# Two batches of keys and values made in the first routed block, its router taken from raw rows, and third attention's first inputs loaded one stage sooner

## The reference: four layers of gated attention and gated feed-forward

```python
x = x + tanh(g_xattn[0]) * L0_xattn(norm(x), ctx, ctx, mask, wq, wk, wv, wo, bo)   # 16 heads of 16
x = x + tanh(g_ffn[0])   * L0_ffn(norm(x), ...)                                   # routed in depth
x = x + tanh(g_xattn[1]) * L1_xattn(norm(x), ctx, ...)
x = x + tanh(g_ffn[1])   * L1_ffn(norm(x), ...)                                   # 8 experts, one each row
x = x + tanh(g_xattn[2]) * L2_xattn(norm(x), ctx, mask, Wq, bq, Wk, bk, Wv, bv, Wo, bo)  # 16 heads of 64
x = x + tanh(g_ffn[2])   * L2_ffn(norm(x), ...)                                   # 16 experts, four each row
x = x + tanh(g_xattn[3]) * L3_xattn(ctx, norm(x))
x = x + tanh(g_ffn[3])   * L3_ffn(norm(x), ...)
```

```python
weights = (x @ router_w)[..., 0] + router_b[0]        # x is norm(x) here
topv, topi = top_k(weights, 16); sel_idx = sort(topi[:, :15])
hn = rmsnorm(x_sel, ln1); q, k = rope(hn @ wq), rope(hn @ wk); ...
x2 = x1 + gelu(rmsnorm(x1, ln2) @ w1) @ w2            # x1 = x_sel + attention
```

## Time and profile before

| | |
|---|---|
| median of 3 runs | 1598.7 us |
| lowest and highest | 1589.78 and 1600.38 us |
| the profiled execution | 1599.66 us |
| its span, first to last instruction | 1597.9 us |
| mean granted TensorE clock | 0.921 |
| PE, PEld, DVE, ACT, POOL busy | 87%, 72%, 53%, 48%, 27% of the span |

### The profile page before, as it was taken

How to read it: one execution, slowest core, us unless ns; L and a number is a source line. 1 busy time by engine, 2 the same in 40 slices (tenths; PEclk the granted TensorE clock), 3 DMA queues, 4 the chain that set the end, 5 groups by cost and what they waited for, 6 DMA issues and landing times. The chain is left out here.

```text
span 1597.9 us, 32065 instructions
## 1 busy us (share of the span) xinstructions
PE 1393.7 (87%) x10658; PEld 1155.8 (72%) x10658; DVE 850.3 (53%) x2171; ACT 767.9 (48%) x1905; POOL 424.3 (27%) x578
## 2 busy tenths in 40 slices
PE   8999878889999999987999999999999998401588
PEld 5888645677799997766888878789999996400355
DVE  4888665766422223005666653832222274688887
ACT  3666453420344435544677673345555522430277
POOL 1000000012122210002333331256666644431141
PEclk9999999899799999998999997889999999755799
DMA  3000020673211126436344432012222343421001
GB/s 108 21 20 15 5 93 1 210 271 64 64 34 39 35 80 208 165 152 215 111 129 143 143 82 93 1 57 94 92 92 93 87 172 128 112 19 10 0 14 40
DMA packets 114518, 140.17 MB, mean 88 GB/s; under 512 B 37072, under 2 KB 93152, under 8 KB 114272
## 3 DMA queue, kind: packets, MB, share of 16 engines
q1 hardware_dynamic: 91872, 85.86, 17.3%
q0 software_dynamic: 11136, 28.93, 6.4%
q10 hardware_dynamic: 11392, 23.86, 4.3%
HBM read 99.96 MB, written 37.49 MB: 86 GB/s over the span
## 5 line engine op out<-in xcount | busy, mean ns | idle before, releaser
L3673 PEld LDWEIGHTS L2f_bank<-L2f_xT,L2f_w_tile 128*128 128x128 f32 x1264 | 154.0, 192 | 7.5 <-ACT L2f_xT L3741 3.5
L3673 PE MATMUL L2f_bank<-L2f_xT,L2f_w_tile 128*128 128x128 f32 x1264 | 154.7, 276 | 3.1 <-ACT L2f_xT L3741 3.1
L3797 DVE TENSOR_TENSOR L2f_hT<-L2f_gate_h,L2f_bank 128x256 f32<-128x256 f32 x79 | 33.3, 421 | 149.1 <-ACT L2f_gate_h L3748 149.1
L906 POOL TENSOR_TENSOR L2x_probs<-L2x_probs,L2x_inv_sum 128x512 f32<-128x512 f32 x64 | 67.8, 1068 | 159.1 <-DVE L2x_inv_sum L1130 159.1
L1047 ACT ACTIVATE L2x_probs<-L2x_shifted,L2x_top 128x128 f32<-128x128 f32 x256 | 99.0, 393 | 14.1 <-DVE L2x_top L1122 14.1
L3596 POOL DMA_INDIRECT L2f_y_rows<-L2f_xn,L2f_put_row x79 | 78.0, 988 | 55.4 <-DVE L2f_xn L3813 51.8
L3735 ACT COPY L2f_w_tile<-L2f_w_up 128x1024 f32 x79 | 82.7, 1047 | 17.7 <-issue 17.7
L3588 POOL DMA_INDIRECT L2f_rows<-L2f_x_rows,L2f_take_row x79 | 76.9, 974 | 45.0 <-DVE L2f_take_row L3561 21.3
L3673 PEld LDWEIGHTS L1f_bank<-L1f_xT,L1f_w_tile 128*128 128x128 f32 x736 | 85.6, 192 | 1.1
L3673 PE MATMUL L1f_bank<-L1f_xT,L1f_w_tile 128*128 128x128 f32 x736 | 85.9, 275 | 0.0
L3690 PE MATMUL L1f_bank<-L1f_w_down,L1f_hT 128*128 x368 | 83.1, 379 | 0.0
(11 more groups left out here) (677 smaller groups left out, 3335.0 us busy)
## 6 DMA issues: line engine op xcount, KB each, us to landing
L1f_w_up<-in_L_ffn_w SPq DMA_DIRECT2D x16, 512.0 KB, 8.6
L1f_w_down<-in_L_ffn_w SPq DMA_DIRECT2D x16, 512.0 KB, 9.3
L2x_k_ahead<-L1f_w_tile ACTq DMA_DIRECT2D x16, 512.0 KB, 2.9
L2x_v_ahead<-L1f_w_tile ACTq DMA_DIRECT2D x16, 512.0 KB, 2.6
L2x_kT<-L2x_k_ahead SPq DMA_DIRECT2D x16, 512.0 KB, 4.6
L2x_v<-L2x_v_ahead SPq DMA_DIRECT2D x16, 512.0 KB, 3.4
L2f_got<-L2f_y_rows SPq DMA_DIRECT2D x16, 512.0 KB, 4.3
L2f_w_up<-in_L_ffn_gate_w SPq DMA_DIRECT2D x16, 256.0 KB, 3.7
```

Of the source, the lines that this page charges most:

```text
L906: nc.gpsimd.tensor_tensor(probs[c][:, :, :], probs[c][:, :, :], inv_sum[:, c, :][:, :, None].to_broadcast([P, 4, P]), ALU.mult).then_inc(s ...
L3673: x = nc.tensor.matmul(products(j, m), w_tile[j][:, at:at + P], xT[j][:, k * P:(k + 1) * P], start=(k == 0), stop=(k == KT - 1))
L3797: nc.vector.tensor_tensor(hT[j][:, 0:F], gate_h[j][:, 0:F], bank[2 + j][:, F:2 * F], ALU.mult).then_inc(q["h"], 1)
```

## The change

1. `DepthLoads` holds the tiles and the loads of the first routed block. They are made before first attention, and SP issues the 16 loads in first attention, after those of batches 2 and 3 and before that of batch 4. The two context batches, `Wk`, `Wv` and `bk` of third attention are among them.
2. The router works on raw rows. In `update` of first attention DVE multiplies the new rows of `x` by the router row and sums (`weigh`), once per batch, after `take_stats`. The sum of the router row is taken once. In the routed block, with r the reciprocal deviation and m the negative mean times r, the score is `raw * r + m * sum(router) + router_b`: three small operations for all batches together.
3. A `KeySite` of 2 batches, 10 pieces, in the routed block. PE fills pieces 0 to 3 in the first phase (0 to 2 ahead of the transposition of the scores), 4 and 5 at the start of the second, 6 and 7 around the second projection, 8 and 9 among the matmuls that spread the result back. They take the place of `stay_warm` there. What stays of it: 1 instead of 11 at the start, the 2 after the transposition, those between the scores and `weighted(0)`, and the last 4. The results are spread back through 6 banks instead of 8.
4. `key_tail` makes 14 batches, 70 pieces.
5. `WideLoads` holds `wq`, `bq`, the gated bias, the masks and the first key tile of third attention. SP loads them at the end of the second routed block, behind the loads of the key site; when the last expert tile is done it also loads `wo`, `bv` and `bo` into the place of the experts' weights. DVE sums the bias there after the experts' results, PE adds the rows in the middle of the key pieces, and DVE makes the gated bias.
6. Third attention starts with both halves of the first queries, then both scores; nothing of the bias is left in it. PE waits for `wo` before the first batch's body.

The core of the diff:

```diff
+class DepthLoads:
+    def load(self, sp):
+        sp.dma_start(self.router_row[:, :], ...).then_inc(s["router"], 16)
+        sp.dma_start(self.router_b[:, :], ...)
+        sp.dma_start(self.pos_in[:, :], ...)
+        sp.dma_start(self.attn_mask[:, :, :], ...)
+        for n, name in enumerate(("wq", "wk", "wv", "wo")):
+            sp.dma_start(self.w4[:, n, :, :], ...)
+        sp.dma_start(self.w1[:, :, :], ...)
+        sp.dma_start(self.w2[:, :, :], ...)
+        for name, dst in (("ln1", self.ln1), ("ln2", self.ln2)):
+            sp.dma_start(dst[:, :], ...)
+        for dst, name in ((self.wk, "wk"), (self.wv, "wv")):
+            sp.dma_start(dst[:, :, :], ...)
+        sp.dma_start(self.bk[:, :], ...)
+        for i in range(2):
+            sp.dma_start(self.rows[i][:, :], ins["ctx_1024"][self.keys.made + i]).then_inc(s["weights"], 16)
+    def weigh(self, dve, j, b):
+        self.core.nc.vector.scalar_tensor_tensor(self.junk[j][:, :], cols(self.core.x, b * D, D), 1.0, self.router_row[:, :],
+                                                 ALU.mult, ALU.mult, accum_out=cols(self.weight, b, 1)
+                                                 ).then_inc(self.sems["weighed"], 1)
...
 (narrow_attention, sync)
-            with sp.Fori(1, B // 2) as i:
+            for j in range(2):
+                body(j, 2 + j)
+            depth.load(sp)
+            with sp.Fori(2, B // 2) as i:
                 for j in range(2):
                     body(j, i * 2 + j)
+            depth.all_in(sp)
 (narrow_attention, vector: update)
                 take_stats(core, b)
+                dve.wait_ge(depth.sems["router"], 16)
+                depth.weigh(dve, j, b)
...
-            update(B - 2)
+            update(0, B - 2)
+            sum_router()
             take_heads(1, B - 1)
-            update(B - 1)
+            update(1, B - 1)
 (depth_routed_block, first phase, tensor)
-            stay_warm(core, bank[7], 11)
+            stay_warm(core, bank[7], 1)
+            site.fill(pe, 0, bank[3], None)
+            site.fill(pe, 1, bank[6], None)
+            site.fill(pe, 2, bank[7], None)
             pe.wait_ge(s["weight"], 1)
...
             pe.wait_ge(s["aug"], 2)
+            pe.wait_ge(s["xn"], B)
...
             pe.wait_ge(s["U_out"], 1)
+            pe.wait_ge(site.s["out"], 3)
...
-            stay_warm(core, bank[0], 1)
+            site.fill(pe, 3, bank[0], None)
+            pe.wait_ge(s["places_read"], 1)
 (first phase, scalar: the order is now)
             finish_norm_scalar(core, act, s, temps)
+            site.empty(act, 0, bank[3])
...         (x_aug of 16 batches, masked)
+            site.empty(act, 1, bank[6])
+            site.empty(act, 2, bank[7])
...         (pickT)
+            site.empty(act, 3, bank[0])
 (first phase, vector)
+            nc.vector.tensor_tensor(weight[:, :], weight[:, :], core.rstd[:, :], ALU.mult)
+            link(nc.vector.tensor_scalar(mean_part[:, :], core.neg_mean_rstd[:, :], depth.router_sum[:, :],
+                                         depth.router_b[:, :], ALU.mult, ALU.add))
+            link(nc.vector.tensor_tensor(weight[:, :], weight[:, :], mean_part[:, :], ALU.add))
-            for b in range(B):
-                dve.wait_ge(s["xn"], b + 1)
-                after(dve, s["weighed"], b - 1)
-                nc.vector.scalar_tensor_tensor(junk[b % 2][:, :], x_aug[:, b, 0:D], 1.0, router_row[:, :],
-                                               ALU.mult, ALU.mult, accum_out=cols(weight, b, 1)).then_inc(s["weighed"], 1)
 (second phase, tensor)
-            stay_warm(core, bank[1], 2)
+            site.fill(pe, 4, bank[1], None)
+            site.fill(pe, 5, bank[2], None)
             pe.wait_ge(t1["hn"], 1)
+            pe.wait_ge(site.s["out"], 4)
             transpose_rows(hn)
             pe.wait_ge(t1["hT_out"], 1)
+            pe.wait_ge(site.s["out"], 6)
...
-            stay_warm(core, bank[3], 2)
+            site.fill(pe, 6, bank[3], None)
             project(1)
-            stay_warm(core, bank[3], 2)
+            site.fill(pe, 7, bank[2], None)
...
-                after(pe, t1["updated"], b - 7)
+                after(pe, t1["updated"], b - 5)
+                if b in (6, 9):
+                    n = 8 + (b == 9)
+                    site.fill(pe, n, bank[n - 2], None)
 (second phase, scalar)
             square(chosen, 0, t1["chosen"])
+            site.empty(act, 4, bank[1])
+            site.empty(act, 5, bank[2])
             take_hT(0)
...
+            site.empty(act, 6, bank[3])
             square(x1, 1, t1["x1"])
             take_hT(1)
+            site.empty(act, 7, bank[2])
...         (four times gelu)
+            site.empty(act, 8, bank[6])
+            site.empty(act, 9, bank[7])
 (routed_experts)
-            site = KeySite(core, "key_tail", keys, B, ...
+            site = KeySite(core, "key_tail", keys, B - keys.made, ...
...
                     site.fill(pe, n, key_bank(n), n - 4 if n >= 4 else None)
+                    if n == n_pieces - 10:
+                        wide.add_rows(pe, wide_rows, bank[0])
...
                 site.load(sp)
+                wide.load(sp)
+                sp.wait_ge(q["down"], S)
+                wide.load_bias(sp, wide_wo, wide_bv, wide_bo)
...         (vector, after the experts' results)
+                wide.sum_bias(dve, wide_wo, wide_bv, wide_rows)
+                wide.make_bias(dve, wide_bo, bank[0])
 (wide_attention, sync and gpsimd at the start)
-            load_mask(0, 0)
-            load_keys(0, 0)
-            for name, dst in (("bq", bq), ("bv", bv)):
...
             load_values(0, 0)
-            load_mask(1, 1)
             load_keys(1, 1)
...
-            for k in range(KT):
-                pool.dma_start(wq[:, k, :], w2d("wq")[k * P:(k + 1) * P, :]).then_inc(s["w_q"], 16)
 (tensor)
-                if first:
-                    pe.wait_ge(s["bv_wo"], KTL)
-                    nc.tensor.matmul(back_bank[:, 0:D], ...).then_inc(s["bv_row"], 1)
-                    pe.wait_ge(s["bv_row"], 2)
             stay_warm(core, out_bank, 2)
-            pe.wait_ge(s["w_q"], 16 * KT)
             front(0, 0, 1)
+            front(0, 0, 2)
             scores(0, 0, 0)
-            front(0, 0, 2)
             scores(0, 0, 1)
+            pe.wait_ge(s["w_o"], 16)
 (vector)
             invert(0, 0)
-            sum_bias()
```

244 lines of the change are left out of this document (149 added, 95 removed).

## The result

| | before | after |
|---|---|---|
| median | 1595.2 us (4 runs) | 1571.3 us (4 runs) |
| lowest and highest | 1589.8 and 1600.4 us | 1568.4 and 1578.9 us |
| the profiled execution | 1599.7 us | 1568.4 us |
| its span, mean granted clock | 1597.9 us, 0.921 | 1566.7 us, 0.929 |

The ratio is 0.985, 95% interval 0.982 to 0.988: 24 us faster by the medians. The forecast was 1572 us. Two later groups of runs gave 0.983 (0.978 to 0.988) and 0.983 (0.980 to 0.986) for the same kernel, 26 and 28 us by the medians.

A forecast was written before the change was run, and what follows sets the result against it. Every stage was taken as bound by something else: PE in the key tail and first attention, a chain over all engines in the first routed block. Terms of -26.6 us from 1599.7 gave 1573.1, adjusted to the median 1572; range 1563 to 1584 us.

The forecast's parts named there:

- Key tail: Second routed block's tail: two batches fewer at 7.23 us each, less 0.5 for bias rows; -14.0 us.
- First attention: First attention: the router's sum on DVE is covered in steady batches, uncovered after the last; +0.4 us.
- Cover: some 5 us: First attention's load queue: early loads in at about 46, batch 4's context and mask wanted at 51.93; cost 0.
- First phase: First routed block, start: scores turned 5.6 us sooner, less 0.8 us waiting for ACT's key halves; -4.8 us.
- Second phase: First routed block, queries and keys: value pieces replace identities and keep PE at high clock; -1.3 us.
- end of the block: First routed block, spreading of results: value pieces replace identities that ran at low clock; -0.4 us.
- Third attention: Third attention's start: early loads let queries begin sooner and the bias work leaves; second batch's queries 6.5 us sooner.
- Low clock: Rival: new PE gaps in third attention and around the picks bring 1.2 GHz; 6 us, 1578 us; chance 0.13.
- DVE as the bound of first attention: Rival: DVE's added 0.35 to 0.51 us a batch is not covered; up to 7 us, 1579 us; chance 0.10.
- The rhythm of the steady batches: Rival: steady batches swallow third attention's gain; only the loads' 3 us survive, 1576 us; chance 0.07.
- The pieces on the path: Rival: all ten key and value pieces run serially in the first routed block; 33 us longer, 1612 us; chance 0.03.
- The queue's case: Rival: slow early loads hold back batch 4 in first attention, PE stands some 29 us; 1601 us; chance 0.04.

The follow-up runs named there:

- the run with three sums: Changed kernel with DVE taking the router's sum of each batch three times in first attention instead of once; median 1572.6 us.
- the reordered version: Changed kernel with scores turned between key halves; in third attention, second query half before the shift and five gap identities added; 1567.4 us, later 1568.0 us.

## Why the prediction was right, step by step

The sum was -26.6 us and the mean of the profiles gives about -25; the medians of the three groups of runs give 24, 26 and 28. The terms:

- **Key tail, -14.0.** Measured -14.8 between means; 7.23 us a batch held to the digit. The bias rows cost 0.4. Right; the other 0.8 us is less than the 0.9 by which the two profiles of before differ.
- **First attention, +0.4.** The batches kept 10.03 and 10.28 us in every run with one sum. What is left after the last batch is less than the stage's scatter of 6 us. That DVE's cover would hold was right. "Cover: some 5 us" for the queue was wrong: 1.0 to 2.4 us. I took the loads to be in at 46; SP issued batch 4's context only at 48.0, and that was the step that failed. The value 0 came out right all the same, narrowly.
- **First phase, -4.8.** 20.7 and 21.7 us before, 18.2, 16.5 and 18.1 after: -3.6 between the means. "K1 ends at 201.2" meant 5.5 us in; it was 5.4 in two of the profiles, 7.1 in one. What failed was the time of the picks: I kept 1.95 us and they took 3.2 to 3.7, at low clock. Where they took 1.95 with the block unchanged, in the run with three sums, the phase was 15.5 us, 5.7 less than the mean before: the path was right and the clock on it was not. The added wait for ACT's key halves, taken as 0.8, was 0.38 there and never bound behind slow picks.
- **Second phase, -1.3, and end of the block, -0.4.** The block's second phase took 74.6 and 72.0 us before and takes 71.7, 70.9 and 73.1: -1.4 between the means, against -1.7, with the ranges overlapping. The eight matmuls behind V0 and V1 took 3.70 us, the high clock as forecast, in all eleven profiles with these pieces. Without them they took 5.40 in two profiles of three and 3.70 in the other, the second of before, behind the same idle stretches of 0.99 and 0.67 us. So an idle stretch of that kind doesn't always bring the low level; the pieces seem to keep it away, and 1.7 us is what that is worth where it would have come. The term as a whole is inside the scatter of the phase.
- **The block as a whole, -6.5.** -5.1 in the mean; single pairs of profiles give anything from -2.5 to -8.
- **Third attention, -6.5.** 6.3 us at the third body in the first profile, 7.0 in the second, 3.7 in the third. The size was right, its parts were not: loads -3.0 and bias -5.7 less what the chain keeps was the sum, and the runs showed 4.8 for loads and order together, and 1.5 for the bias. The forecast "the next shift comes 4.4 us later because of the sum" was right (4.7 in the run that put it back), but 3 us of it were waits behind it.
- **Rivals.** Low clock was given 0.13 as a case by itself. It is not a case but happened somewhere in each of the three executions of after: in the picks, in the second batch's queries (4.29 us instead of 3.74 in the first profile), in the last projections. Its price was also worked out wrong: 64 matmuls at twice 0.117 us are 7.5 us more, not 3. DVE as the bound of first attention fell at one sum and began to hold at three. The rhythm of the steady batches took 1.6 us of the 7.9 that the second body had gained, not all but 3. The pieces on the path fell: no pieces gave the same block. The queue's case fell, by 1 us of cover.

The forecast of 1572 against 1571 is closer than its terms deserve. The third routed block, of which nothing was said, and the tail gave 2.4 us more, first attention, first block and third attention 4.5 us less. And it was counted down from 1598.7, the median of three runs of the kernel before; with the fourth that is 1595.2, from which the same sum would have given 1568.6. That part is luck.

## What to carry to other kernels

Work moved into another stage's gaps costs by what it makes late: ten matmul groups here cost nothing that could be seen once the scores were ready early, and the same ten stood beside a 5 us hole and 2.8 us of low clock while the scores came late; look at what PE does between the moved work and the next wait. A sum moved off the path is worth its length less the waits that stood behind it on the same engine, so read those rows first. And where single stages differ by up to 6 us between two executions of one kernel, cut several profiles of each kernel at the same instruction before explaining a difference of 2 us.

## What the runs showed of the hardware that I had not expected

- The same instructions at the start of the kernel ran at a mean granted clock of 0.85, 0.90 or 1.00 from one execution to the next; the first statistics came 3.8 us apart (43.3 and 47.1 us).
- PE was busy without a gap for 6.3 us up to the broadcast of the places in the first profile of the reordered version, and idle for only 0.58 us since, and still the picks behind took 3.49 us against 1.95 in the second profile of the same program, with the same rows ahead of them. How densely PE was used just before did not fix the level by itself.
- The issue of a load can hold SP for long: 9.1 us for two transfers of 128 KB behind 15 others, and 11.8 us with 2 MB more ahead of them.
